# Factor splits of the effective weights moved half a group ahead, in a gated cross-attention block

## The reference

```
x = x + tanh(g_xattn) * attention(layernorm(x), ctx, Wq, Wk, Wv, Wd)
x = x + tanh(g_ffn)   * ffn(layernorm(x), gate, up, down)

# each ffn linear multiplies its weight by a factor of rank 4 first
w_eff = w * (su @ sv)
y     = x @ w_eff.T
d     = silu(gate(x)) * up(x);  out = down(d)
```

## Time and profile before

| | us |
|---|---|
| median of three runs | 1487.97 |
| the profiled execution | 1488.45 |
| its span | 1486.6 |
| PE busy | 1458.5 |
| DVE, ACT, POOL busy | 1100.4, 640.0, 828.0 |

### The profile page before, as it was taken

How to read it: one execution, slowest core, us unless ns; L and a number is a source line. 1 busy time by engine, 2 the same in 40 slices (tenths; PEclk the granted TensorE clock), 3 DMA queues, 4 the chain that set the end, 5 groups by cost and what they waited for, 6 DMA issues and landing times.

```text
span 1486.6 us, 20638 instructions
## 1 busy us (share of the span) xinstructions
PE 1458.5 (98%) x7322; PEld 1185.6 (80%) x7322; DVE 1100.4 (74%) x1581; ACT 640.0 (43%) x1115; POOL 828.0 (56%) x724
## 2 busy tenths in 40 slices
PE   8999999999999999999999999999999999999998
PEld 8878788888888777777777777777888888888886
DVE  5366777777677777777777778878488887767676
ACT  5445455454444343443343444434344444333332
POOL 5598999998788112111121332234387877666663
PEclk9999999999999999999999999999999999999999
DMA  8476687778987633334333333342012111311121
GB/s 271 153 231 216 217 261 247 251 248 302 330 294 248 240 114 114 114 121 137 125 114 114 114 115 137 135 158 66 22 46 62 43 57 50 121 43 63 45 59 69
DMA packets 116070, 218.02 MB, mean 147 GB/s; under 512 B 9472, under 2 KB 47616, under 8 KB 113920
## 3 DMA queue, kind: packets, MB, share of 16 engines
q1 hardware_dynamic: 115968, 216.70, 43.6%
HBM read 151.13 MB, written 65.54 MB: 146 GB/s over the span
## 4 chain that ended last, share of the span: by engine, by line
PE 85%; DVE 6%; ACT 4%; issue 3%; DMA 1%; POOL 1%; SPq 0%; DVEq 0%; ACTq 0%; POOLq 0%
PE bank L535 65%; PE bank L652 4%; ACT o_hi L1010 3%; PE bank L813 3%; PE bank L812 3%; PE bank L814 3%; PE bank L699 2%; PE bank L679 2%; DVE el L1214 1%; DVE er L1214 1%; PE bank L579 1%; DVE X L1376 1%; DMA c_raw<-in_ctx_t 1%; PE bank L723 0%; DVE xc L1208 0%
## 5 line engine op out<-in xcount | busy, mean ns | idle before, releaser
L1546 POOL TENSOR_TENSOR wd_lo<-wd_raw,wd_hi 128x512 fp32r<-128x512 f32 x64 | 94.9, 1501 | 400.8 <-ACT wd_hi L979 400.8
L535 PE MATMUL bank<-xc,wa_hi 128*128 128x512 f32 x896 | 277.3, 391 | 0.0
L535 PE MATMUL bank<-wd_hi,o_hi 128*128 128x512 f32 x512 | 202.1, 395 | 7.6 <-ACT o_hi L1010 7.6
L535 PE MATMUL bank<-wd_hi,o_lo 128*128 128x512 f32 x512 | 199.7, 390 | 0.0
L535 PE MATMUL bank<-wd_lo,o_hi 128*128 128x512 f32 x512 | 199.3, 389 | 0.0
L535 PEld LDWEIGHTS bank<-xc,wa_hi 128*128 128x128 f32 x896 | 167.7, 188 | 36.0 <-issue 1.1
L535 PE MATMUL bank<-xc,wa_lo 128*128 128x512 f32 x448 | 174.5, 390 | 0.0
L1376 DVE SCALAR_TENSOR_TENSOR X<-bank,tg,X 128x512 f32<-128x512 f32 x224 | 156.4, 741 | 0.0
L1301 DVE TENSOR_TENSOR o_lo<-bank,o_hi 128x512 fp32r<-128x512 f32 x128 | 82.1, 684 | 99.7 <-ACT o_hi L1010 99.7
L535 PE MATMUL bank<-x_hi,wf_hi 128*128 128x512 f32 x392 | 153.1, 391 | 0.0
L535 PE MATMUL bank<-x_hi,wf_lo 128*128 128x512 f32 x392 | 152.6, 389 | 0.0
(11 more groups left out here) (176 smaller groups left out, 3393.3 us busy)
## 6 DMA issues: line engine op xcount, KB each, us to landing
q_scratch<-q_st SPq DMA_DIRECT2D x32, 1024.0 KB, 4.3
q_sb<-q_scratch SPq DMA_DIRECT2D x64, 512.0 KB, 5.8
w_raw<-in_wq SPq DMA_DIRECT2D x32, 512.0 KB, 4.1
wd_raw<-in_wd SPq DMA_DIRECT2D x16, 1024.0 KB, 5.2
f_raw<-ffn_eff_scratch SPq DMA_DIRECT2D x28, 512.0 KB, 3.6
er_raw<-in_sf_r SPq DMA_DIRECT2D x42, 256.0 KB, 3.9
e_raw<-in_wf SPq DMA_DIRECT2D x42, 256.0 KB, 5.3
ffn_eff_scratch<-e_eff SPq DMA_DIRECT2D x42, 256.0 KB, 5.1
```

Source lines behind the costliest of these rows:

```text
L535: last = pe.matmul(to, a, b, start=(start and n == 0), stop=(stop and n == 3 * len(pairs) - 1), skip_group_check=onto)
L1546: g.tensor_tensor(wd_lo[h % 2][:, e, :], wd_raw[:, e, :], f32(wd_hi[h % 2][:, e, :]), ALU.subtract).then_inc(g_wd, 1)
```

## The change

In the stream of ACT the high parts of the factors of group q + 1 come at the end of group q (behind L967, ahead of the scaling of x), and the combinations move from ahead of L967 to behind it. In the stream of DVE the low parts of group q + 1 come at the end of group q, behind the effective weight and ahead of `x_lo` and `stats1`. Only group 0 still makes its own in its middle. On SP the factors' loads go ahead of those of the left operand. On POOL the power goes ahead of `c_combinations_lo` in the groups up to 7, and in group 8 ahead of `left_sums`.

```diff
@@ quad_dmas
             if q + 6 < len(LOADS):
                 load_c(q + 6)
+            if q in E_AT and m + 1 < NP:
+                load_lr(m + 1)
             if q in (NV - 4, NV - 3):
                 load_w(q - NV + 4)
             if w == 0:
                 load_w(2)
             if 0 <= w and w + 3 < NW:
                 load_w(w + 3)
-            if q in E_AT and m + 1 < NP:
-                load_lr(m + 1)
@@ scalar, quad
-            if q in E_AT:
-                lr_hi(E_AT[q])
+            if q == 0:
+                lr_hi(0)
...
-            if q + 2 < NCH:
-                c_combinations(q + 2)
...
             a.activation(result(q, 0, 0), split(q, bank[0][:, :]), ACT.Copy).then_inc(a_c11, 1)
+            if q + 2 < NCH:
+                c_combinations(q + 2)
+            if q + 1 in E_AT:
+                lr_hi(E_AT[q + 1])
             if q in APPLY:
                 apply1(APPLY[q])
@@ vector, quad
-            if q in E_AT:
-                lr_lo(E_AT[q])
+            if q == 0:
+                lr_lo(0)
...
             if q in E_AT and q < NQ - 2:
                 effective(E_AT[q])
+            if q + 1 in E_AT:
+                lr_lo(E_AT[q + 1])
             if q in X_SPLIT:
                 x_lo(X_SPLIT[q])
@@ gpsimd
             if q + 2 < NCH:
                 c_sums(q + 2)
+            if q < NV and q in APPLY:
+                ln_pow(APPLY[q])
+            if q + 2 < NCH:
                 c_combinations_lo(q + 2)
             if 0 <= w + 1 < NW:
                 left_lo(w + 1)
+            if q == NV and q in APPLY:
+                ln_pow(APPLY[q])
             if 0 <= w + 2 < NW:
                 left_sums(w + 2)
-            if q in APPLY:
+            if q > NV and q in APPLY:
                 ln_pow(APPLY[q])
```

## The result

The changed kernel takes 1491.99 us (median of 10 runs, 1489.57 to 1493.38) where the kernel before takes 1487.78 (10 runs, 1487.15 to 1489.85). The ratio is 1.0024, with a 95% interval of 1.0014 to 1.0034: **0.24% slower**, 1.7 us above the forecast of 1490.3. The profiled execution of the changed kernel took 1492.22 us, its span is 1490.4 (before: 1488.45 and 1486.6).

The account below looks back on a forecast made before the run. PE bounds the kernel, busy for 1458.5 of 1486.6 us, so only its waits count. 1488.45 - 2.9 + 5.6 - 0.4 = 1490.75 for the profiled execution, 0.48 above the median: 1490.3 us, range 1487.5 to 1493 (with rivals 1484.0 to 1495.5).

Parts of the forecast that it names:

- The rule of the shared stretch: DVE operations with two SBUF tensors and POOL's operations wait for each other, turn by turn; `stats1`, with one input, isn't held.
- Groups 0 to 3: Wait on L967 and slow clock go, 3.65 us; `t1` costs 1.2; group 4 gives back what group 1 won.
- Groups 5 to 13: Power ahead of the left operand's sums in group 8; group 12 stands 2.9 us sooner, ends 1.2 and 4.1.
- `s5` behind `x_hi`: On ACT's queue in groups 3 and 6: `s5` comes late for PE, 0.9 us each time.
- Groups 15, 19, 23 and 27: `x_lo` waits for POOL's tile of 1024, `t1` behind it holds PE: 1.4 us each, 5.6 us slower in sum.
- rival (b): Slow clock follows the new waits in groups 4, 15, 19, 23, 27: 1.7 us per fall, 1495.4 us, chance 0.18.
- the prediction's own signs of being wrong: `x_lo` still near 2.1 us, no wait on `t`, or a granted clock under 1 behind 200 us.
- POOL's tile of 512 can't start sooner or much later: In groups 14, 18, 22, 26: it waits for `left_hi`, which waits for product 3; start taken as 216.96.
- The rest: Factors' loads delay others only by their issue: nothing, or an estimated 1 us without cover; group 42 wins 0.30 and 0.12.
- Group 43: `er` leaves the chain to the first transposes of probabilities in group 42, 0.30 and 0.12 won; group 43 itself 0.
- Rival (a): The change works everywhere, `x_lo` taking its turn ahead of the tile of 1024: 1483.0 us, chance 0.14.
- rival (c): The change doesn't act, low parts still waiting for ACT's copies or a DMA; gain and loss near 1 us: 1488 us, chance 0.11.

Follow-up runs that it names:

- The exchange of the two steps: The changed kernel with `x_lo` put ahead of `lr_lo` on DVE, both still ahead of the next `t1`: 1491.65 us, ratio 1.0029.
- the narrow tile: The changed kernel with POOL's third tile cut from 1024 to 128 columns in four `left_lo` calls: 1483.15 us, ratio 0.9967.
- the loads first: The changed kernel with the factors' loads issued on SP ahead of `store_e` and `load_e` from group 10 on: 1490.96 us, ratio 1.0019.

## Why the prediction was right in sign, and where its terms were off

**The rule of the shared stretch held.** It is the step on which all hung. The exchange of the two steps (the loser changes, the bill doesn't) and the narrow tile (4.11 to 2.17 us) show it directly. The Trainium skill's GPSIMD Engine Reference, section Specifications, agrees in kind; that the turns are of whole instructions is read from these rows. `stats1` wasn't held, as predicted, but not every operation with one input is free: in the kernel before, DVE's scaling of two columns in SBUF, issued 0.05 us behind POOL's tile of 1024, ended with it, where it takes 0.2 to 0.3 us in most groups. First DVE (the two statistics, then the scaling), then POOL:

```profile
142.38 1.27 DVE L1188 BATCH_NORM_STATS2 bn<-x_st 128x6 f32<-128x512 f32 x2
...
144.65 2.37 DVE L1197 TENSOR_SCALAR veps<-moments 128x2 f32<-128x2 f32 x1
```

```profile
142.65 1.99 POOL L1540 TENSOR_TENSOR wa_lo<-w_raw,wa_hi 128x512 fp32r<-128x512 f32 x2
144.60 2.40 POOL L1540 TENSOR_TENSOR wa_lo<-ws,wa_hi 128x1024 fp32r<-128x1024 f32 x1
```

**Groups 0 to 3: right.** The wait on `v_st` and the slow clock are gone, the effective matmul of group 1 stood at 73.45 (73.5 predicted), and group 4 gave most of it back by a wait on `t` of 2.32 (2.6 predicted). `s5` was late by 0.4, not 0.9. The 73.45 agrees partly by offset: `t1` of group 1 came when it was predicted, but PE stood 0.6 us later than priced, as group 0 did, and so waited 0.33 us for it and not 1.2.

**Groups 5 to 13: right in kind, 2.2 us too small** (5.1 for 2.9). Group 9 stood at 158.71 for 160.0. Two terms were mis-sized. `s5` behind `x_hi`, taken at 0.9 in groups 3 and 6, measured 0.37 and 0.36, which is 1.1 us. The new waits of groups 10 and 11, taken at 0.5 and 1.2, were 0.36 in all, while the old ones that they were set against went: another 0.9 or so (the lead grew from 4.4 to 5.1 there, where -0.2 had been taken). The upper end given, 4.1, was passed.

**Groups 15, 19, 23 and 27: right in kind, 3.0 us too small** (8.6 for 5.6). The steps were all there, `x_lo` at 4.1 us and `t1` behind it; groups 19 and 23 cost 1.4 and 1.3 for 1.4. What was missing:
- The slow clock behind the wait in group 15: 1.7 us. That is rival (b)'s mechanism in one place out of five. It had been given a chance, but as a case of at least two falls; and a granted clock under 1 behind 200 us was one of the prediction's own signs of being wrong, which did come. Its bracket doesn't hold either: the 2.6 us priced for group 4 doesn't lie between 1.64 and 1.83, and the measured 2.32 there brought no fall.
- Group 15's wait was 2.40 for 1.65, +0.7. The step that failed is "POOL's tile of 512 can't start sooner or much later, since it waits for `left_hi`". The tile started 216.96 - 214.38 = 2.6 us behind the effective matmul before, but 212.89 - 209.31 = 3.6 after, and it waited for POOL's own sums, which ran right up to it, 1.1 us beyond the end of the copy L916. The larger lead of PE isn't the reason, as the two halves show. With combinations and power alone (first pair: effective matmul of group 14, then POOL's tile) PE is 6.2 us ahead and the distance is 2.6, as before; with the factors alone (second pair) PE is 3.0 ahead and it is 3.5:

```profile
208.20 0.40 PE L579 MATMUL bank<-er,el 96*128 96x512 f32 x1
210.78 3.78 POOL L1540 TENSOR_TENSOR wa_lo<-w_raw,wa_hi 128x512 fp32r<-128x512 f32 x2
```

```profile
211.40 0.40 PE L579 MATMUL bank<-er,el 96*128 96x512 f32 x1
214.91 2.05 POOL L1544 TENSOR_TENSOR wa_lo<-w_raw,wa_hi 128x512 fp32r<-128x512 f32 x2
```

  **The early factors made POOL later against PE**, and this place was priced from the distance of before. POOL was already late in group 11: its sums started 8.9 us behind the effective matmul with the early factors (with or without the other half) and 7.0 without them. That this comes from the turns with `er` and `x_lo` in group 10 is likely, but no run shows it.
- Group 27's wait was 2.19, +0.7, by the late load. The step that failed is in "The rest": it prices only what the factors' loads delay ("The other loads have a group's length of cover: nothing") and has no term for when they land themselves, behind `store_e` and `load_e`, for an ACT that now needs them half a group sooner. ACT's waits on them went to 45.8 us. Most show no wait of PE behind them; one does, and some 0.5 us went in groups 35 to 38, where PE's waits follow ACT's `s` (0.4) and DVE's `t` (0.3) behind such loads.

**Group 43: right**, 0.4.

The errors of the two large terms, +2.2 and -3.0, and the 0.5 cancelled in part: by them 1490.75 becomes 1490.75 - 2.2 + 3.0 + 0.5 = 1492.05, and the profiled execution took 1492.22. The median came out 1.7 us above the forecast and inside its own range of 1487.5 to 1493, but by sizes that offset each other: the mechanism held, the nearness of the number is luck in part.

Rival (a), works everywhere, fell with `x_lo` at 4.11 us; rival (c), doesn't act, with the leads of +2.5 and +5.1.

## What to carry to other kernels

Before moving a step within an engine's queue, write down who waits for the step behind it: 11.7 us lay here between `x_lo` ahead of and behind the next `t1`. An instruction that takes turns with another engine's can cost that engine's longest instruction on top of its own time (4.11 us for 2.09 here), so put it where nothing urgent is queued behind it, or make the other's instruction shorter. A change can also shift the engines against each other, here POOL by 1 us against PE: price the later places from the new distances, the landing of loads among them. And try the halves of a change alone: one half of this one gained 6.3 us and the other lost 6.7.

## What the runs showed of the hardware

The granted clock didn't follow the length of the wait alone. It fell to the lower level behind a wait of 1.83 us, but not behind one of 1.84 in the same place with the factors alone:

```profile
57.00:75.00 18.00, 16.16 (x71) 1.00 0.57 184
```

It fell behind waits of 2.28 to 2.40 in group 15 in all five profiles that had one. In group 4 it fell behind 2.31 with the loads first and behind 2.52 with `x_lo` ahead of `lr_lo`, but not behind the same 2.31 and 2.32 in three other profiles; never behind the waits of 1.39 to 2.19 in groups 19, 23 and 27. What tells these apart stays open; a fall that the profile priced took 3.4 us at the lower level and cost 1.7.
